# Transposing the identity into waiting PSUM banks: half of each planned gap of TensorE in a decoder layer

## The reference, cut to what matters

```
x = x + attention(layernorm(x))          # 16 heads of 32, causal softmax, w_qkv, w_o
x = x + ssm(ctx, z=layernorm(x))         # Mamba block: in_proj, conv of 4 taps + silu, x_proj -> dt, B, C,
                                         # scan over 512 positions for 512 channels x 16 states,
                                         # y + D*u, times silu(z)
x = x + ffn(layernorm(x))                # layer norm, absmax fake-quant, ternary w_fc (2048 x 512), exact gelu,
                                         # layer norm, fake-quant, ternary w_proj (512 x 2048)
```

## Time and profile before

| | |
|---|---|
| median of three executions | 1187.19 us |
| the profiled execution, whole | 1185.84 us |
| its span, first to last instruction | 1184.0 us |
| TensorE busy | 989.5 us, 84% |
| VectorE busy | 973.8 us, 82% |
| ScalarE busy | 833.8 us, 70% |
| GpSimd busy | 633.6 us, 54% |
| mean granted TensorE clock | 0.914 of full |

### The profile page before, as it was taken

One profiled execution on the slowest core, in us unless ns is written; L12 is line 12 of the kernel. 1 busy time (PEld: TensorE's weight loads), 2 busy tenths in 40 slices (PEclk: granted clock), 3 DMA queues, 4 the chain that ended last, 5 costly groups with the idle time before them and its releaser, 6 DMA issues.

```text
span 1184.0 us, 17538 instructions
## 1 busy us (share of the span) xinstructions
PE 989.5 (84%) x5268; PEld 737.2 (62%) x5268; DVE 973.8 (82%) x1351; ACT 833.8 (70%) x1579; POOL 633.6 (54%) x510
## 2 busy tenths in 40 slices
PE   5757989799888998898899767585799898989896
PEld 2325766559655676655677555474577676878775
DVE  4677689895799976997988789899899989998554
ACT  3763787865696765897876887747989778974342
POOL 1246456864528757546664933468555556543301
PEclk8969999799998998998999877787699999999899
DMA  5304755434345651433463351430110110000000
GB/s 185 108 19 125 221 153 161 124 116 153 90 125 164 189 166 61 137 109 121 124 201 108 104 211 29 147 120 9 49 50 32 37 32 29 26 14 19 10 19 18
DMA packets 59355, 115.82 MB, mean 98 GB/s; under 512 B 8880, under 2 KB 13232, under 8 KB 58240
## 3 DMA queue, kind: packets, MB, share of 16 engines
q1 hardware_dynamic: 59264, 114.70, 31.5%
HBM read 90.42 MB, written 24.25 MB: 97 GB/s over the span
## 4 chain that ended last, share of the span: by engine, by line
PE 46%; DVE 24%; issue 11%; ACT 10%; POOL 7%; DMA 0%; DVEq 0%; SPq 0%; POOLq 0%; ACTq 0%
PE ps L1661 8%; PE ps L1729 7%; PE ps L1810 5%; DVE hb L1830 5%; PE ps L1742 5%; DVE y_acc L1852 4%; PE ps L1675 4%; PE ps L1701 4%; PE ps L1800 2%; POOL hb L1261 2%; DVE du L1882 2%; PE ps L1714 2%; PE ps L1687 2%; DVE hb L1838 2%; PE ps L1632 2%
## 5 line engine op out<-in xcount | busy, mean ns | idle before, releaser
L1261 POOL TENSOR_TENSOR hb<-du,b_bc 128x1024 f32<-128x1024 f32 (+1 forms) x160 | 319.6, 2017 | 183.7 <-PE ps L1729 180.2
L1830 DVE TENSOR_TENSOR_SCAN hb<-ps,hb 128x1024 f32<-128x1024 f32 (+1 forms) x128 | 257.8, 2015 | 31.8 <-ACT ps L1390 19.9
L1390 ACT ACTIVATE ps<-delta,a_neg 128x511 f32<-128x511 f32 (+2 forms) x320 | 180.3, 598 | 92.1 <-DVE hb L1830 84.4
L1729 PE MATMUL ps<-ident,hb 128*128 128x128 f32 x1088 | 173.6, 305 | 52.2 <-DVE hb L1830 31.4
L1852 DVE SCALAR_TENSOR_TENSOR y_acc<-ps,ct,y_acc 128x512 f32<-128x512 f32 x256 | 183.3, 742 | 39.1 <-PE ps L1729 37.4
L1729 PEld LDWEIGHTS ps<-ident,hb 128*128 128x128 f32 x1088 | 140.2, 157 | 83.2 <-DVE hb L1830 39.0
L1505 ACT ACTIVATE p_q<-ps,m_col 128x512 f32<-128x512 f32 (+3 forms) x256 | 131.4, 526 | 21.3 <-DVE m_col L1924 20.0
L1661 PE MATMUL ps<-xn_t,w_ring 128*128 128x512 f32 x256 | 122.0, 621 | 6.3 <-ACT p_t L1521 2.6
L1800 PE MATMUL ps<-t_fc,xq_hi 128*128 128x512 f32 x256 | 111.2, 434 | 9.6 <-DVE xq_lo L2038 5.6
L1810 PE MATMUL ps<-t_pr,hq_hi 128*128 128x512 f32 x256 | 104.6, 409 | 8.3 <-DVE hq_lo L2038 5.3
L1521 ACT ACTIVATE p_t<-ps 128x512 f32<-128x512 f32 x160 | 86.6, 600 | 32.0 <-PE ps L1701 31.7
(11 more groups left out here) (152 smaller groups left out, 1994.6 us busy)
## 6 DMA issues: line engine op xcount, KB each, us to landing
w_ring<-in_w_attn SPq DMA_DIRECT2D x32, 512.0 KB, 4.2
qk_d<-hl SPq DMA_DIRECT2D x64, 256.0 KB
q_st<-qk_d SPq DMA_DIRECT2D x128, 128.0 KB, 2.8
b_bc<-bc_d SPq DMA_DIRECT2D x48, 256.0 KB, 3.8
k_st<-qk_d SPq DMA_DIRECT2D x64, 128.0 KB, 2.6
k_st<-qk_d SPq DMA_DIRECT2D x128, 64.0 KB, 2.3
x_in<-in_x SPq DMA_DIRECT2D x16, 256.0 KB, 3.6
raw_fc<-in_w_fc SPq DMA_DIRECT2D x4, 1024.0 KB, 8.7
```

The costliest lines, as they stand in the source:

```text
L1261: nc.gpsimd.tensor_tensor(piece_of(e, hi, lo).rearrange("p (a n) -> p a n", a=2), du[b % 2][:, 2 * h:2 * h + 2, lo:hi], b_bc[:, i % BC_RIN ...
L1390: ins = nc.scalar.activation(factors(j, hi, lo)[:, (hi - lo) * m + start:(hi - lo) * (m + 1)], delta[b % 2][:, et, lo + start:hi], ACT.Exp ...
L1729: mm = nc.tensor.transpose(bank(kind, *a)[:, P * et:P * et + P], piece_of(2 * r + et // 2, hi, lo)[:, at:at + P], ident[:])
L1830: v.tensor_tensor_scan(h, d, h, 0.0, ALU.mult, ALU.add).then_inc(scan_done, 1)
```

## The change

`plan()` now notes for each item of TensorE that fills a bank how long the engine stands still in the plan while a bank is already empty: `at - max(room, free)`. Half of that (`FILL`), in units of 0.11 us (`FILL_US`) and rounded down, is the item's number of fills. In TensorE's stream a new helper `stand_by` runs ahead of each item (ahead of the first half alone for `rot`, `v` and `wo`): it makes the wait on the bank, which used to stand behind the item's data waits, and then issues that many transposes of `ident` into the bank's first 128 columns. Nobody reads them, since the item's own matmuls overwrite the bank. The block that picks the bank moves ahead of the update of `free` in `plan()`, which leaves the order and the places as they were.

```diff
+FILL, FILL_US = 0.5, 0.11
...
-    turns, place = [], {}
+    turns, place, fill = [], {}, {}
...
         out[engine].append(item)
+        if (engine, item) in last_use:
+            room, n = bank()
+            fill[item] = int(FILL * max(0.0, at - max(room, free[engine])) / FILL_US)
+            place[item] = n, held[n][-1] if held[n] else None
+            held[n].append(last_use[engine, item])
...
-        if (engine, item) in last_use:
-            n = bank()[1]
-            place[item] = n, held[n][-1] if held[n] else None
-            held[n].append(last_use[engine, item])
...
-    return out, place
+    return out, place, fill
...
-ORDER, PLACE = plan()
+ORDER, PLACE, FILLS = plan()
...
+            def stand_by(*item):
+
+
+                bank_free(*item)
+                for _ in range(FILLS[item]):
+                    nc.tensor.transpose(bank(*item)[:, 0:P], ident[:], ident[:])
+
             for kind, *a in ORDER["pe"]:
                 first = kind == "first"
                 if first:
                     kind, *a = a[0]
+                if first or kind not in W_KINDS:
+                    stand_by(kind, *a)
                 if kind == "ln1b":
                     b, t = a
                     n, i = TASK[kind, b, t], LT * b + t
                     pe.wait_ge(ln1_done, i + 1)
-                    bank_free(kind, *a)
...
```

More of the change, by code:

```diff
@@ L716, in plan @@
         out[engine].append(item)
+        if (engine, item) in last_use:
[3 more added lines that the diff above has]
+            held[n].append(last_use[engine, item])
+            if item[0] in ("xt", "ht_ffn"):
+                for who in ("act", "dve") if turns else ():
+                    before[who, item] = before[who, item] + [(who, turns[-1])]
+                turns.append(item)
         if engine == "sp":
@@ L1682, in _ @@
                     pe.wait_ge(stack_in[p % 2], 160 * (p // 2 + 1))
-                    bank_free(kind, p, n)
                     dst = bank(kind, p, n)
```

## The result

The changed kernel takes 1173.44 us (median, 1171.79 to 1177.48) beside 1187.03 for the kernel before on the same chip: ratio 0.9893, interval 0.9877 to 0.991. The profiled execution took 1174.1 us, its span is 1172.3.

The account below looks back on a forecast made before the run. TensorE and VectorE, handing work to each other, were taken as the bound, with TensorE's clock falling behind gaps. Eight terms summed to -5.0 us: profiled 1185.84 to 1180.8, median 1182.2, own range 1178 to 1185, with rivals 1177.5 to 1191.

Parts of the forecast that it names:

- Rival (d): Whole kernel: identity transposes don't count as work for the clock, so fills only cost time; 1196 us, chance 0.05.
- rival (a): Whole kernel: planned gaps aren't TensorE's, most falls only come a little later and fills delay; 1191.1 us, chance 0.15.
- Rival (c): Whole kernel: more clock comes back, at 158 to 233 us and `xproj` 2 in full, fewer falls after; 1177 us, chance 0.07.
- It removes no wait.: Whole kernel: the change can only keep the clock up or lengthen TensorE's work; no term for waits.
- Part 7: 677 to 840 us: fills around `wtot` give -1.1, those of `t` 31 and `fc` 1 zero; -1.6 us in all.
- Part 1: Head: 28 fills ahead of the first matmul cost 3.2 us, a fall avoided near 21 us returns 2.1; +1.1 us.
- Part 3: 80 to 120 us: fills ahead of `ht` 3 and `ht` 4 keep the clock up, 1.3 and 1.7 back; -2.8 us.
- Part 4: 158 to 233 us: small fills cost 0.6, the 14 ahead of `s` 8 taken as -0.5; +0.1 us.
- Part 2: 42 to 79 us: 84 fills hidden behind ScalarE, `xproj` 1 still at half clock; 0 us.
- part 5: `xproj` 2: 8 fills shorten the gap ahead of it, half of the 2.8 us lost to slow clock returns; -1.4 us.
- part 6: Ten single fills up to 580 us, half of them on the chain; +0.5 us.
- part 8: The end: 6 fills at 1130 us cost 0.7, the 18 ahead of `proj` 14 bring back 1.6; -0.9 us.

Follow-up runs that it names:

- fills_old_waits: Kernel before with the fills; only items that have fills wait for their bank early, the others keep data, then bank: 1178.22 us, ratio 0.9941.
- both_waits: Kernel before with the bank wait made twice, ahead of the data waits and behind them as before, no fills: 1187.46 us, ratio 1.0015.
- part 6 of the experiments: Three kernels without gap fills: bank wait moved only up to about 410 us (0.9992), only from there (0.9953), everywhere with four transposes added there (1.0002).
- waits_only: Changed kernel with every fill dropped, the bank wait still ahead of the data waits: 1181.13 us, ratio 0.9955 to the kernel before.
- no_wtot: Changed kernel without the 31 fills ahead of `ht` 53, `wtot` 1, `ht` 54 and `wo` of the last batch: 1177.45 us, ratio 0.9921.
- no_fc1: Changed kernel without the 35 fills ahead of `fc` 1: 1173.01 us, ratio 0.9877 to the kernel before.
- no_head: Changed kernel without the 67 fills ahead of the first three `inproj` items: 1169.35 us, ratio 0.986 to the kernel before.
- the best version: Changed kernel with 645 fills at 31 places from the kernel before's trace, none ahead of the first three `inproj`: 1165.86 us, ratio 0.9819.
- late_only: Changed kernel with fills only ahead of `t` 27 and later items, the moved wait kept throughout: 1175.16 us, ratio 0.9907 to the kernel before.
- waits_early: Kernel before, no fills, bank wait ahead of the data waits only for items up to `s` 16 (about 410 us): 1185.88 us, ratio 0.9992.
- waits_delay: Moved bank wait everywhere and no fills, but four transposes (0.45 us) once ahead of `s` 16: 1186.4 us, ratio 1.0002 to the kernel before.
- head4: Kernel before with four transposes of the identity ahead of its first matmul, all waits as before: 1186.28 us, ratio 1.0002.

## Why the prediction was off, step by step

The sign and the mechanism were right: fills hold the clock, and the mean clock rose, by 0.039 where about 0.016 was forecast. Rival (d), that the identity doesn't count as work, is refuted by `fills_old_waits` and the rows at 1.00 behind the fills; rival (a), that the falls only move, by the four filled gaps behind which the clock is now 1.00 (24 to 31, 119 to 122, 772 to 786 and 1150 to 1157 us). Rival (c), 1177, came nearest: it had parts 4 and 5 in full, and the trace has 2.2 us for each. The number fell outside the range for the following reasons, largest first.

**"It removes no wait."** This step failed. The forecast gave the moved wait no term at all. It is worth 5.3 us alone (0.9955), 5.7 with the fills in place (0.9893 beside 0.9941), and nothing when the old check stays (`both_waits`, 1.0015). The fills alone measured 0.9941 (0.9925 to 0.9957), that is 7.0 us (5.1 to 8.9), against the forecast's 5.0: without the missing term the forecast would have been 2.0 us off. Had it been priced as the time of the wait, it would have come to some tenths of a microsecond; the larger steps are the clock's (part 6 of the experiments).

**Part 7, -1.6 us; measured -5.6 between `t` 27 and `proj` 0.** The fills of `wtot` and `ht` 53 and 54 were taken at 1.1 us and measured 3.3 to 4.0. The pieces that the forecast counted are right, the `ht` of 1.97 us is 1.09, and `wo` starts its 64 matmuls 5 us earlier than before. Two things were left out. The moved wait is in the 5.6: `waits_only` gains 3.2 between the same two places with no fill at all. And the lead that the fills give doesn't end where VectorE is dense: from the end of `wo` 3 to `proj` 0 after gains another 3.1 us, `no_wtot` none. Its two zeros were right: `t` 31's fills left a gap of 3.16 us, and the clock falls behind it still (0.50 from 757.6 to 761.0 us); `fc` 1's bring nothing (`no_fc1`).

**Part 1, +1.1 us; measured +3.1.** The 28 fills were priced at the full level (3.2 us) with 5.9 in brackets. TensorE has done nothing before them, and they took 6.11 us. The `inproj` behind them is then at full speed, so ScalarE's first read came at 15.61 us, 4.25 later than before and not 3.2. The 2.1 us that should come back were 1.2 by `xproj` 0. Leaving the 67 fills out saves 3.9 us (`no_head`), so the term's sign was right and its size too small. That it was a third is less sure: kernels with nothing ahead of their first matmul lie anywhere from 0.04 us early to 1.64 late at `xproj` 0.

**Part 3, -2.8 us; measured -1.4.** `ht` 4's 1.7 us came back whole, as its row shows. At `ht` 3 the fills left 2.26 us of the gap, and the records behind it are slow still (12 transposes in 2.63 us, 8 matmuls in 4.21): 1.3 out of the bounds 0 to 1.7 was the wrong choice, the lower bound the right one.

**Part 4, +0.1 us; measured -2.2.** The clock in the fills of `s` 8 is 0.51 as forecast, but of the 7.60 us of work at half level 3.40 are left, and the fills themselves are 3.2 of them: the kernel's own work there is at full level again, `ht` in 1.06 us and not 1.97. That is the forecast's other end, -2.3.

**Part 2, 0; part 5, -1.4; part 6, +0.5; part 8, -0.9.** `xproj` 1 stayed slow (6.20 us) and the offset of the program hardly changed between 40 and 80 us. `xproj` 2 went from 6.38 to 5.21 us, 1.2 of the 1.4; the table has 2.2 earlier between `s` 8 and there. From `xproj` 2 to `t` 27, part 6's stretch, the trace has -0.7, and `waits_only` -1.7: less that, the single fills cost 1.0. At the end the 6 fills at 1130 us cost 0.55 us (forecast 0.7) and `proj` 14 gained 1.5 (1.6). The rest of the 2.5 us between `proj` 0 and `proj` 15 lies ahead of them, and `waits_only` gains 1.6 there too.

**"Gaps under 2 us have none."** This reading, under rival (a), was wrong. In the kernel before, five of the 29 slow stretches have no gap of 2 us in them or in the 6 us ahead; the first of these, by stretches and in the timeline:
```profile
208.80:215.60 6.80, 5.93 (x25) 0.50 0.48 173
```
```profile
209.28 1.11 PE L1729 MATMUL ps<-ident,hb 128*128 128x128 f32 x4 [1.12 <-DVE hb L1830]
```

Two rules of the Trainium skill were weighed, both of TensorE: Matmul & The Clock Gate, "Part 1: The HAM clock gate". The sentence that the ramp costs "<1% of a typical kernel span" stands there for the ramp at the start of a kernel. For that the trace agrees: the 28 first fills took 6.11 us where 3.2 is their time at full level, 2.9 us of 1172.3. The forecast took it as the price of all falls, and that it isn't: the rows give 204.8 us of 1184.0 at the half level, and the best version, with 118.9 us less of it, takes 1.8% less time. That the place where the clock changes isn't tied to the start of the kernel agrees with the head: the same eight matmuls took 5.36 to 6.35 us in four executions of the same instructions (`late_only`, `waits_early`, `waits_only`, `waits_delay`). Behind the head little of it shows: in `both_waits` and `head4` the slow stretches stand as much later as the work, and of 19 runs of the kernel before beside them most have a mean clock of 0.914, all 0.909 to 0.922. At 0.909 the run took 1188.95 us, at 0.922 1183.43, so single falls do come and go between runs of one kernel, within some 3 us of the median; four runs of the changed kernel spread over 5.7 us. Both are less than what the change moved.

## What to carry to other kernels

Where the clock falls at gaps, price a change by the slow stretches that it can start or end, and not only by the microseconds that it moves: here 0.45 us was worth 5.3 us. Ask of each stretch whether it lies on the path, since 12.8 us less of slow time in `waits_delay` and 6.8 us at `fc` 1 gave nothing. Place fills by the measured trace, nearly the whole gap (4.9 us better than half of the planned gap, both without the head), never ahead of an engine's first work, and with instructions that fill the time. And read the diff for the waits that it reorders: such a change can be worth much more, or less, than the time of the wait. One profile beside another is no measure for 2 us; the medians are.

## What the runs showed of the hardware

- In the first microseconds the view of stretches shows a granted clock of 1.00 while the instructions take twice as long: 28 transposes in 6.11 us, 0.21 each, the same form at 0.113 later. There the durations tell the level, the clock column doesn't; the sums of slow time above leave that out.
- Where the clock first rises differs between executions of the same instructions (eight matmuls in 5.36 to 6.35 us). Behind the head the slow stretches near 465 us of `both_waits` and `head4` stood at the same work as in the kernel before: 1.2 and 2.1 us later, with the work 1.2 and 2.2 us later.
- A fall doesn't need one long gap: 208.8 to 215.6 us of the kernel before is at 0.50 behind a gap of 1.12 us.
- 28 transposes of 16 x 16 took 0.91 us, 28 of 128 x 128 6.11, both at the head; a matmul of fp32 with two columns is two records and took 12.11 us for 28, twice the full transpose.
